# First batch's layer norm by halves, with loads, sums and low parts of the first three batches in another order

## The reference, cut to what matters

```
h = max(layernorm(x), 0)
A = [adj, adj, shifted, adj^T, adj^T, shifted^T, eye]
HW[r]  = h @ W[r, :F] + W_edges[r] @ W[r, F:]
out    = max over r of (A[r] @ HW[r]) + b
return x + out
```

```
eye     = zeros_like(A1) + jnp.eye(N)
shifted = jnp.roll(eye, 1, axis=0)
```

## Time and profile before

| | us |
|---|---|
| median of 3 runs | 217.32 |
| lowest and highest | 216.86, 217.63 |
| the profiled execution's own time | 216.98 |
| its span | 215.3 |
| PE busy | 206.3 (96%) |
| DVE busy | 177.0 (82%) |
| ACT busy | 160.8 (75%) |
| POOL busy | 95.9 (45%) |
| mean share of the DMA engines in q1 | 64.3% |

### The profile page before, as it was taken

One profiled execution on the slowest core, in us unless ns is written; L12 is line 12 of the kernel. 1 busy time (PEld: TensorE's weight loads), 2 busy tenths in 40 slices (PEclk: granted clock), 3 DMA queues, 4 the chain that ended last, 5 costly groups with the idle time before them and its releaser, 6 DMA issues.

```text
span 215.3 us, 3420 instructions
## 1 busy us (share of the span) xinstructions
PE 206.3 (96%) x902; PEld 149.5 (69%) x902; DVE 177.0 (82%) x414; ACT 160.8 (75%) x431; POOL 95.9 (45%) x140
## 2 busy tenths in 40 slices
PE   7799779999999999999999999999999999999994
PEld 7456456777767777777767777776777777777772
DVE  3574997988889797988989798888979798888755
ACT  3779788697896969698796969689696969876220
POOL 3112946446172735527082644617273552718200
PEclk9999979999999999999999999999999999999998
DMA  5999995376693939678492938769393938610101
GB/s 175 313 345 370 376 362 199 108 292 245 202 336 93 380 79 313 215 253 283 156 355 69 374 127 295 241 198 335 86 384 89 342 130 253 234 53 0 50 0 49
DMA packets 31587, 47.14 MB, mean 219 GB/s; under 512 B 1632, under 2 KB 11088, under 8 KB 31568
## 3 DMA queue, kind: packets, MB, share of 16 engines
q1 hardware_dynamic: 31568, 46.92, 64.3%
HBM read 42.72 MB, written 4.19 MB: 218 GB/s over the span
## 4 chain that ended last, share of the span: by engine, by line
PE 84%; SPq 6%; DMA 5%; DVE 2%; issue 1%; ACT 1%; POOL 0%; DVEq 0%; ACTq 0%; POOLq 0%
PE bank_p L761 11%; PE bank_p L763 10%; PE bank_p L762 9%; PE bank_g L725 6%; PE bank_gT L704 6%; PE bank_g L730 5%; PE bank_g L729 5%; PE bank_g L736 5%; DMA adj_sb<-in_adj_dram 5%; PE bank_gT L716 5%; PE bank_gT L710 5%; PE bank_gT L709 4%; PE bank_p L751 3%; PE bank_p L679 3%; PE bank_p L671 3%; PE bank_g L762 2%
## 5 line engine op out<-in xcount | busy, mean ns | idle before, releaser
L321 POOL TENSOR_TENSOR a_lo<-adj_sb,a_hi 128x512 fp32r<-128x512 f32 x15 | 19.4, 1295 | 72.3 <-DVE h_lo L548 68.5
L579 DVE TENSOR_TENSOR best<-bank_p,best 128x512 f32<-128x512 f32 x48 | 33.2, 691 | 8.4 <-PE bank_p L763 7.3
L434 ACT ACTIVATE gT_hi<-bank_gT 128x512 fp32r<-128x512 f32 x16 | 9.6, 598 | 30.9 <-PE bank_gT L716 30.5
L576 DVE SCALAR_TENSOR_TENSOR best<-bank_p,c_col,best 128x512 f32<-128x512 f32 x32 | 24.0, 750 | 5.8 <-ACT best L453 5.1
L389 ACT ACTIVATE a_hi<-adj_sb 128x512 fp32r<-128x512 f32 x45 | 27.7, 620 | 1.3 <-DMA adj_sb<-in_adj_dram 1.3
L402 ACT ACTIVATE aT_hi<-adjT_sb 128x512 fp32r<-128x512 f32 x45 | 27.7, 620 | 0.0
L315 POOL TENSOR_TENSOR o_sb<-best,x_bias 128x512 f32<-128x512 f32 x15 | 20.0, 1332 | 15.8 <-DVE best L579 15.8
L418 ACT ACTIVATE h<-x_sb,shift,rstd 128x128 f32<-128x128 f32 x60 | 24.7, 497 | 1.4 <-DVE shift L528 1.4
L542 DVE TENSOR_TENSOR aT_lo<-adjT_sb,aT_hi 128x512 fp32r<-128x512 f32 x30 | 24.5, 854 | 0.0
L729 PE MATMUL bank_g<-aT_hi,h_hi 128*128 128x512 f32 x45 | 24.4, 541 | 0.0
L709 PE MATMUL bank_gT<-a_hi,h_hi 128*128 128x512 f32 x45 | 23.6, 525 | 0.0
(11 more groups left out here) (110 smaller groups left out, 501.8 us busy)
## 6 DMA issues: line engine op xcount, KB each, us to landing
adj_sb<-in_adj_dram SPq DMA_DIRECT2D x15, 1024.0 KB, 5.6
adjT_sb<-in_adjT_dram SPq DMA_DIRECT2D x15, 1024.0 KB, 5.6
xT_sb<-in_xT_dram SPq DMA_DIRECT2D x16, 256.0 KB, 5.9
x_sb<-in_x_dram SPq DMA_DIRECT2D x15, 256.0 KB, 6.1
out_dram<-o_sb SPq DMA_DIRECT2D x15, 256.0 KB, 5.9
adj_sb<-in_adj_dram SPq DMA_DIRECT2D x4, 256.0 KB, 3.4
adjT_sb<-in_adjT_dram SPq DMA_DIRECT2D x4, 256.0 KB, 4.8
w_sb<-in_W_dram SPq DMA_DIRECT2D x3, 128.0 KB, 4.5
```

What stands on the lines that cost most here:

```text
L579: op = nc.vector.tensor_tensor(best[q][:, :], product, best[q][:, :], ALU.max)
```

## The change

The two halves of the first x are issued by ScalarE's queue and no longer by SyncE's. The first batch's statistics, scale, shift and h are made in two halves, each with semaphores of its own; ScalarE now makes three chunks of h and VectorE one. TensorE does the first aggregation before it turns h, each chunk as soon as its h is there, behind 7 warm-up matmuls where there were 10. SyncE's loads of adj(2), adjT(2) and x(3) change places among those of bias, xT and x. VectorE and ScalarE do the low and high parts of batch 0 in another order; `split_adj_lo(1)` stands ahead of `variance(2)` and of `take_best(0, 2)`. `part_sums(1)` stands ahead of `split_adjT_last(1)` on GpSimd. The c terms of the last product are issued with the other c terms of the last batch, and `turn_sums(0)` follows products 3 and 4.

```diff
-WARM_UP = 10
+WARM_UP = 7
-        last_banks = (bank_g, bank_p[1])
+        last_banks = (bank_g, bank_p[0])
 SyncE
-            for i in range(2):
-                half = slice(i * HALF, (i + 1) * HALF)
-                sp.dma_start(x_sb[0][:, half, :], x_dram[0][:, half, :]).then_inc(x0_in[i], 16)
...
             load_x(2)
+            load_adj(2)
             sp.dma_start(bias_sb[:, :], biasT).then_inc(bias_in, 16)
             load_xT(0)
+            load_adjT(2)
             load_xT(1)
-            for b in range(B):
+            load_x(3)
+            for b in range(1, B):
+                if b + 1 < B:
+                    load_xT(b + 1)
                 if b + 3 < B:
                     load_x(b + 3)
                 if b + 2 < B:
                     load_adj(b + 2)
-                if b > 0:
-                    store(b - 1)
+                store(b - 1)
                 if b + 2 < B:
                     load_adjT(b + 2)
-                    load_xT(b + 2)
 GpSimd
             add_bias(0)
+            part_sums(1)
             split_adjT_last(1)
             add_bias(1)
             for b in range(1, B):
-                part_sums(b)
                 finish(b - 1)
...
                     split_adjT_last(b + 1)
+                    part_sums(b + 1)
 ScalarE
+            for i in range(2):
+                half = slice(i * HALF, (i + 1) * HALF)
+                act.dma_start(x_sb[0][:, half, :], x_dram[0][:, half, :]).then_inc(x0_in[i], 16)
...
-            std_of(0)
+            act.wait_ge(half_aggr_done, 1)
+            nc.scalar.activation(std[:, 0:HALF], mean_var[0][:, 0:HALF, 1], ACT.Sqrt,
+                                 bias=eps[:, :]).then_inc(half_std_ready, 1)
+            act.wait_ge(half_shift_ready, 1)
+            for c in range(HALF):
+                nc.scalar.activation(h[0][:, c, :], x_sb[0][:, c, :], ACT.Relu, bias=shift[:, c:c + 1],
+                                     scale=rstd[:, c:c + 1]).then_inc(half_h_ready, 1)
+            act.wait_ge(aggr_done, 1)
+            nc.scalar.activation(std[:, HALF:], mean_var[0][:, HALF:, 1], ACT.Sqrt,
+                                 bias=eps[:, :]).then_inc(std_ready, 1)
...
-            split_hT(0)
...
             split_gT(0)
+            split_hT(0)
 VectorE
+            def first_variance(i, stats_sem, aggr_sem):
+                dve.wait_ge(x0_in[i], 16)
...
+            def first_scale_and_shift(i, std_sem, rstd_sem, shift_sem):
...
-            split_hT_lo(0)
             dve.wait_ge(wh_in, 32)
             nc.vector.tensor_copy(w_hi[:, :NH, :], w_sb[:, :NH, :]).then_inc(whi_ready, 1)
+            split_gT_lo(0)
+            split_hT_lo(0)
+            variance(1)
+            dve.wait_ge(wa_in, 32)
+            nc.vector.tensor_copy(w_hi[:, NH:, :], w_sb[:, NH:, :]).then_inc(whi_ready, 1)
+            scale_and_shift(1)
             dve.wait_ge(c_psum, 1)
...
-            variance(1)
-            split_gT_lo(0)
-            dve.wait_ge(wa_in, 32)
-            nc.vector.tensor_copy(w_hi[:, NH:, :], w_sb[:, NH:, :]).then_inc(whi_ready, 1)
-            scale_and_shift(1)
             split_g_lo(0)
             take_best(0, 1)
             split_h_lo(1)
+            split_adj_lo(1)
             variance(2)
-            take_best(0, 2)
-            split_adj_lo(1)
-            for i in range(NH, NPROD):
+            for i in range(2, NPROD):
                 take_best(0, i)
 TensorE
                 for i in range(NH, NPROD - int(b == B - 1)):
                     add_sums(i, bank_of[i], start=True)
+                if b == B - 1:
+                    pe.wait_ge(best_begun, B)
+                    for nodes, to in zip(HALVES, last_banks):
+                        add_sums(NPROD - 1, to, nodes, start=True)
...
-                turn_sums(0)
                 pe.wait_ge(gTlo_ready, 1)
                 pe.wait_ge(wlo_ready, 2)
                 passes(3, bank_of[3][:, 0:N], start=True)
                 passes(4, bank_of[4][:, 0:N], start=True)
+                turn_sums(0)
                 product(0, 2)
...
-            turn_h(0)
             aggregate_T_first()
+            turn_h(0)
...
-            pe.wait_ge(best_done, (B - 1) * NBEST + 1)
             for nodes, to in zip(HALVES, last_banks):
-                add_sums(NPROD - 1, to, nodes, start=True)
                 product(B - 1, NPROD - 1, nodes, to)
```

More of the change, by code:

```diff
@@ L157, in gnn_kernel @@
         aggr_done = sem("aggr_done")
+        half_stats_done = sem("half_stats_done")
+        half_aggr_done = sem("half_aggr_done")
+        half_std_ready = sem("half_std_ready")
+        half_rstd_ready = sem("half_rstd_ready")
+        half_shift_ready = sem("half_shift_ready")
+        half_h_ready = sem("half_h_ready")
         std_ready = sem("std_ready")
@@ L458, in _ @@
             act.wait_ge(eps_ready, 1)
-            std_of(0)
+            act.wait_ge(half_aggr_done, 1)
[8 more added lines that the diff above has]
+                                 bias=eps[:, :]).then_inc(std_ready, 1)
             act.wait_ge(shift_ready, 1)
-            for c in range(HALF):
-                last = nc.scalar.activation(h[0][:, c, :], x_sb[0][:, c, :], ACT.Relu,
-                                            bias=shift[:, c:c + 1], scale=rstd[:, c:c + 1])
+            for c in range(HALF, C - 1):
+                last = nc.scalar.activation(h[0][:, c, :], x_sb[0][:, c, :], ACT.Relu, bias=shift[:, c:c + 1],
+                                            scale=rstd[:, c:c + 1])
             last.then_inc(h_ready, 1)
-            split_hT(0)
             for c in range(C):
@@ L505, in variance @@
                 for c in range(C):
-                    if b == 0 and c % HALF == 0:
-                        dve.wait_ge(x0_in[c // HALF], 16)
-                    elif b > 0 and c == 0:
+                    if c == 0:
                         dve.wait_ge(x_in[b % NX], x_loads(b))
@@ L518, in variance @@
                 last.then_inc(aggr_done, 1)
+            def first_variance(i, stats_sem, aggr_sem):
+                dve.wait_ge(x0_in[i], 16)
+                for c in range(i * HALF, (i + 1) * HALF):
+                    last = nc.vector.bn_stats(stats[:, c, :], x_sb[0][:, c, :])
+                last.then_inc(stats_sem, 1)
+                dve.wait_ge(stats_sem, 1)
+                nc.vector.memset(wait_carrier[:, :], 0.0)
+                for c in range(i * HALF, (i + 1) * HALF):
+                    last = nc.vector.bn_aggr(mean_var[0][:, c, :], stats[:, c, :])
+                last.then_inc(aggr_sem, 1)
+            def first_scale_and_shift(i, std_sem, rstd_sem, shift_sem):
+                half = slice(i * HALF, (i + 1) * HALF)
+                dve.wait_ge(std_sem, 1)
+                nc.vector.reciprocal(rstd[:, half], std[:, half]).then_inc(rstd_sem, 1)
+                dve.wait_ge(rstd_sem, 1)
+                nc.vector.scalar_tensor_tensor(out=shift[:, half], in0=mean_var[0][:, half, 0], scalar=-1.0,
+                                               in1=rstd[:, half], op0=ALU.mult, op1=ALU.mult).then_inc(shift_sem, 1)
             def scale_and_shift(b):
                 dve.wait_ge(std_ready, b + 1)
-                if b >= 1:
-                    dve.wait_ge(h_ready, b)
+                dve.wait_ge(h_ready, b)
                 if b == 1:
@@ L586, in _ @@
             nc.vector.tensor_reduce(row_lo[:, :], groups[:, :, 2:4], AXIS.XY, ALU.add).then_inc(masks_ready, 1)
-            variance(0)
-            scale_and_shift(0)
+            first_variance(0, half_stats_done, half_aggr_done)
+            first_scale_and_shift(0, half_std_ready, half_rstd_ready, half_shift_ready)
+            first_variance(1, stats_done, aggr_done)
+            first_scale_and_shift(1, std_ready, rstd_ready, shift_ready)
             dve.wait_ge(shift_ready, 1)
[L590 to L593, removed]
+            nc.vector.tensor_scalar(h[0][:, C - 1, :], x_sb[0][:, C - 1, :], rstd[:, C - 1:], shift[:, C - 1:],
+                                    ALU.mult, ALU.add).then_inc(h0_scaled, 1)
             dve.wait_ge(h0_scaled, 1)
-            nc.vector.tensor_scalar(h[0][:, HALF:, :], h[0][:, HALF:, :], 0.0, None, ALU.max).then_inc(h0_ready, 1)
+            nc.vector.tensor_scalar(h[0][:, C - 1, :], h[0][:, C - 1, :], 0.0, None, ALU.max).then_inc(h0_ready, 1)
             dve.wait_ge(blocks_ready, 1)
@@ L665, in turn_h @@
                 pe.wait_ge(h_ready, b + 1)
-                if b == 0:
-                    pe.wait_ge(h0_ready, 1)
-                else:
+                if b >= 1:
                     pe.wait_ge(best_done, (b - 1) * NBEST + 1)
@@ L686, in aggregate_T_first @@
                     pe.wait_ge(adj0_in[c], 16)
+                    if c < HALF:
+                        pe.wait_ge(half_h_ready, c + 1)
+                    elif c < C - 1:
+                        pe.wait_ge(h_ready, 1)
+                    else:
+                        pe.wait_ge(h0_ready, 1)
```

(2 more changed lines are left out.)

## The result

The changed kernel took 219.39 us in the median of 12 runs (218.78 to 220.14), the kernel before 217.21 (12 runs, 216.53 to 218.63). The ratio is 1.0096, with an interval of 1.0076 to 1.0117: slower by 2.1 us. The forecast was 218.9, in 216.2 to 219.9, with 0.57 for slower. The profiled execution took 219.19, and its span is 217.5, for 215.3 before: +2.2.

The account below looks back on a forecast made before the run. TensorE, busy 206.3 of 215.3 us, was taken as the bound, setting the pace alone from product(1, 0). Gate +0.7, clock +1.3 and end −0.1 gave +1.9 us on 216.98: 218.9, range 216.2 to 219.9.

Parts of the forecast that it names:

- the gate: Start of product(1, 0) on TensorE, after which TensorE alone sets the pace: about 33.9 instead of 33.18, +0.7 us.
- the clock: TensorE at 1.2 GHz after idling 2.2 us before product(1, 0): +1.3 us, bounds 0 and 1.7.
- the end: Last product's c terms go first, but VectorE's three maxima limit the gain: −0.1 us, bounds −0.2 and +0.1.
- Two chains at the gate: TensorE's half-speed chain and VectorE's chain reached product(1, 0) together before; earlier idle and clock cost mostly hidden, some 0.1 to 0.2 us.
- the late x(3): x(3), loaded behind adj(2) and adjT(2), lands at 27.9, so VectorE's variance(3) starts 0.4 us later.
- GpSimd's blocking: finish(0) on GpSimd holds the shared port, so VectorE's split_adjT_lo(1) ends 0.4 us later from this; bounds 0 and 0.8.
- The front: First batch: batch 1 arrives 1.2 us earlier on TensorE and VectorE, bounds 0 and 1.9.
- Three warm-up matmuls fewer cost nothing: First batch on TensorE: 7 warm-up matmuls instead of 10 cost nothing, as TensorE waits for h there.
- The wait behind `turn_sums(0)`: First batch on TensorE: the copy of the sums, without products 3 and 4 as cover, is waited for some 0.8 us.
- The loads: x(0) on ScalarE's queue fills a hole in the DMA stream: loads behind gain 0.65 us, bounds 0 and 1.0.

Follow-up runs that it names:

- e10: Changed kernel with the loads in their old order (bias, xT(0), xT(1), x(3), adj(2), adjT(2) behind x(2)); 219.33 us, ratio 1.0092.
- e3: Changed kernel with 11 warm-up matmuls for 7; 218.85 us, ratio 1.0077.
- e9: Changed kernel with the two halves of x(0) back on SyncE's queue, in front of adj(0); 220.04 us, ratio 1.0091.
- e1: Changed kernel with eight matmuls of 512 columns, result overwritten, in TensorE's idle time before product(1, 0); 217.69 us, ratio 1.0032.
- e2: Changed kernel with GpSimd's add_bias(1) and finish(0) moved behind split_adj_last(2); 218.22 us, ratio 1.0051.
- e6: Kernel before with eight matmuls of 512 columns, result overwritten, between turn_h(1) and turn_sums(1); 216.60 us, ratio 0.9978.
- e7: Kernel before with only the two halves of x(0) issued by ScalarE's queue; 219.62 us, ratio 1.0084.

## Why the prediction was right

The sum was +0.7 for the gate, +1.3 for the clock and −0.1 for the end. The spans give +0.70, +1.47 and 0.0. The time was 2.2 above the kernel before, for 1.9.

*Two chains at the gate.* Right: in every version on the changed kernel the gate opens within 0.2 us behind VectorE's low part of the turned h, or behind a filler. The 1.8 us that `part_sums(1)` gained (26.28 for 28.07, forecast 26.3) bought nothing at the gate.

*The gate, +0.7: the size right, the split wrong.* I had 0.4 from the late x(3) and 0.4 from GpSimd's blocking. The trace has 0.0 and 0.71, the upper part of the bound of 0.8 for blocking. The failed step is the one I called the step on which the forecast rests, "`variance(3)` starts 0.4 us later than before, although VectorE was free". x(3) landed at 27.4 (forecast 27.9), but VectorE was not free before 27.5: e10 landed it 5.5 us earlier and changed nothing. e3 and e9 show the mechanism at work as soon as the front is fast, with waits of 1.07 and 2.52 us; the load was the next limit behind the one that acted. That the +0.7 came out is partly luck: the landing was put 0.4 too high and the blocking 0.3 too low.

VectorE's unchanged arrival is a coincidence too. It begins `take_best(0, 1)` 1.08 us later than before (20.44 for 19.36), and catches up in `split_adj_lo(1)`. Before, that pair ran beside GpSimd's operations from 21.30 on; now it comes ahead of `variance(2)`, and GpSimd starts only at 22.38. Before, then after:

```profile
22.33 2.51 DVE L535 TENSOR_TENSOR a_lo<-adj_sb,a_hi 128x512 fp32r<-128x512 f32 x2
...
21.58 1.29 DVE L571 TENSOR_TENSOR a_lo<-adj_sb,a_hi 128x512 fp32r<-128x512 f32 x2
```

*The blocking.* Right: the pair of low parts ends 1.15 us behind `finish(0)`, as I read it from the earlier trace rows, in e1, e3, e9 and e10 it ends 1.15 or 1.16 behind it, and without the two GpSimd operations it takes 1.26 (e2). The Trainium skill ("SBUF — State Buffer", section "SBUF: two separate sides") says that the shared port pair is held for the whole instruction by whichever of a VectorE operation with two SBUF inputs and a GpSimd operation starts first, and that the other blocks; these ends agree.

*The clock.* Right in kind, and e1 shows it: 1.47 us behind the gate, for 1.3, and 1.7 in the medians. The length of idle time alone did not decide what it cost; its place did. In the kernel before, the stretch lay in front of the gate, and the runs without one were no shorter (e6).

*The front: mis-sized, with the wrong sign.* I had batch 1 arrive 1.2 us earlier; it came 1.08 later (22.62 for 21.54). The first aggregation took 5.39 us for its eight matmuls, where e3 has 3.65. In 6.30 to 8.90 three of them took 0.87 each, twice the 0.43 of the same matmul in the fast executions, which is the pace of 1.2 GHz, although the window's clock column has 1.00; a weight load took 0.34 us there, as in the 0.50 stretch behind the gate (0.33), and 0.19 elsewhere. Ahead of it TensorE had worked 3.36 us and then idled 1.36. "Three warm-up matmuls fewer cost nothing" was wrong in this kernel, but they do not cost the 1.7 us alone: e9 has the same seven and an earlier x(0), idled 0.38 us behind them and took 3.70, and e7 has ten and the late x(0), idled 1.70 and took 3.60 in its profiled execution. Only the two together were seen slow. With a fast first aggregation batch 1 came 0.5 us earlier than before (21.03 in e3, 21.04 in e9), within my bounds of 0 and 1.9. The wait behind `turn_sums(0)`, 0.69, was as forecast (0.8).

*The loads.* x(0) on ScalarE's queue comes at 4.07 for 3.02, which I had not costed at all; adj(0), issued at the same moment, shares the engines. The Trainium skill's rule that DMAs of several issuing engines run on the same 16 DMA engines and interleave ("DMA: Bandwidth & Descriptors", section "Issuing engines are not separate DMA queues") agrees with that 1.05 us. On the kernel before, the second queue alone cost time (e7).

*The end.* No gain, for −0.1: as before, VectorE's three maxima set it.

## What to carry to other kernels

Find the instruction where two engines' chains meet before one of them takes over for good, and cost each edit by what it does there; a stall removed ahead of it bought nothing here. Idle time of TensorE right in front of the work that sets the pace cost twice here, once as a wait of 2.0 us and once as 1.47 us in the clock of what followed, while the same wait further ahead was hidden. Before moving a GpSimd operation, see which VectorE operations with two operands in SBUF it will stand beside.

## What the hardware showed that I had not expected

- A load on a second queue was delayed: x(0)'s first half was there 1 us later (3.98 and 4.07 for 3.02) when adj(0) was issued beside it.
- The clock column has 1.00 in 6.30 to 8.90 of the changed kernel while matmuls run at half pace (0.87 us for 0.43). At the start the durations told the pace and the column didn't.
- Matmuls whose result is thrown away made the changed kernel 1.7 us faster (e1).
- The two GpSimd operations made two VectorE operations take 2.38 us for 1.26.
